# Expert slots of 128 rows against 48 whole slots and 20 slots of four 32-row pieces, in an attention-like block with a routed feed-forward part on one core

## The reference, cut to what matters

```python
logits = hidden @ router_w.T                         # 16 experts
top_vals, top_idx = jax.lax.top_k(logits, 1)         # one expert for each token
scores = sigmoid(top value at the chosen expert, -inf elsewhere)
routed_in = hidden[None] * scores.T[:, :, None]
gate, up = split(einsum('nth,nhf->ntf', routed_in, gate_up_proj))   # 128 + 128 columns
routed_out = einsum('ntf,nfh->nth', up * silu(gate), down_proj)
shared = silu(hidden @ shared_gate_w.T) * (hidden @ shared_up_w.T) @ shared_down_w.T   # width 512
out = x + shared + routed_out.sum(axis=0)
```

## Time and profile before

| | |
|---|---|
| median of 3 runs | 490.7 us (490.6 to 490.88) |
| the profiled execution | 490.73 us, span 488.6 us |
| TensorE's mean granted clock | 0.999 |
| TensorE, VectorE, ScalarE, GpSimd busy | 98%, 76%, 66%, 72% of the span |
| HBM | 21.69 MB read, 17.93 MB written |

### The profile page before, as it was taken

The page is one execution under the profiler, slowest core; times in us unless marked ns, Lnnn a source line. Parts: engine busy times, 40 slices in busy tenths (PEclk is TensorE's granted clock), DMA queues, the critical chain, the costliest instruction groups (busy, mean ns, idle before and its releaser), DMA issues.

```text
span 488.6 us, 10463 instructions
## 1 busy us (share of the span) xinstructions
PE 477.0 (98%) x3093; PEld 388.2 (79%) x3093; DVE 371.1 (76%) x1056; ACT 323.8 (66%) x623; POOL 352.3 (72%) x573
## 2 busy tenths in 40 slices
PE   8999999999999999999999999999999999999995
PEld 7655777868777778686777867888899999999995
DVE  7889899899999998997899989747445555555535
ACT  2667887978978879777687886554365555555521
POOL 6655688898888988986788777677236676667750
PEclk9999999999999999999999999999999999999999
DMA  7007001102101011020101101111389854442028
GB/s 238 2 1 281 22 12 56 54 13 66 33 34 65 24 45 54 12 67 21 46 25 41 45 1 44 45 44 37 117 197 225 226 158 136 145 139 76 24 52 294
DMA packets 33031, 39.33 MB, mean 80 GB/s; under 512 B 4913, under 2 KB 29113, under 8 KB 32720
## 3 DMA queue, kind: packets, MB, share of 16 engines
q1 hardware_dynamic: 26640, 24.98, 17.8%
q0 software_dynamic: 5760, 13.16, 7.8%
q10 hardware_dynamic: 576, 0.52, 0.3%
HBM read 21.69 MB, written 17.93 MB: 81 GB/s over the span
## 4 chain that ended last, share of the span: by engine, by line
PE 77%; DVE 6%; issue 5%; POOL 5%; DMA 4%; ACT 2%; SPq 1%; POOLq 0%; DVEq 0%; ACTq 0%
PE bank L427 17%; PE bank L420 9%; PE bank L444 6%; PE bank L414 4%; PE bank L822 3%; PE bank L823 3%; PE bank L815 3%; PE bank L435 3%; PE bank L528 3%; PE bank L514 3%; PE bank L540 3%; PE bank L524 3%; PE bank L519 3%; PE bank L688 2%; PE bank L697 2%
## 5 line engine op out<-in xcount | busy, mean ns | idle before, releaser
L427 PE MATMUL bank<-hT,wm 128*128 128x256 f32 x512 | 124.7, 383 | 0.6 <-ACT kr L908 0.6
L427 PEld LDWEIGHTS bank<-hT,wm 128*128 128x128 f32 x512 | 92.0, 190 | 18.7 <-issue 8.3
L1528 POOL DMA_INDIRECT sorted_rows<-rows,posi x64 | 71.9, 1124 | 19.6 <-issue 16.9
L1612 POOL DMA_INDIRECT out<-shared x55 | 53.2, 967 | 37.3 <-DVE shared L1442 22.3
L420 PEld LDWEIGHTS bank<-wm,k 128*128 128x128 f32 x512 | 61.7, 192 | 7.6 <-issue 6.6
L420 PE MATMUL bank<-wm,k 128*128 128x128 f32 x512 | 62.1, 275 | 0.0
L1084 ACT ACTIVATE er<-bank 128x256 f32<-128x256 f32 x40 | 15.4, 384 | 44.8 <-PE bank L823 44.3
L1450 DVE TENSOR_TENSOR e<-er,bank 128x256 f32<-128x256 f32 x40 | 16.9, 421 | 23.0 <-ACT er L1084 21.1
L444 PE MATMUL bank<-wm,actA 128*128 128x128 f32 x240 | 32.9, 280 | 0.0
L1612 POOL DMA_INDIRECT out<-rows x24 | 23.1, 964 | 11.3 <-DVE rows L1442 5.3
L944 ACT ACTIVATE h<-rows,smE 128x128 f32<-128x128 f32 x64 | 26.3, 482 | 6.7 <-POOL smE L1504 6.7
(11 more groups left out here) (256 smaller groups left out, 1293.9 us busy)
## 6 DMA issues: line engine op xcount, KB each, us to landing
shared<-sorted_rows SPq DMA_DIRECT2D x56, 128.5 KB, 2.9
shared<-x SPq DMA_DIRECT2D x16, 256.0 KB, 3.0
rows<-sorted_rows SPq DMA_DIRECT2D x24, 128.5 KB, 2.5
wexp<-w_exp SPq DMA_DIRECT2D x2, 1536.0 KB, 8.4
sorted_rows<-filler SPq DMA_DIRECT2D x17, 128.5 KB
shared<-out SPq DMA_DIRECT2D x6, 256.0 KB, 4.7
out<-shared SPq DMA_DIRECT2D x12, 128.0 KB, 2.7
sorted_rows<-rows,posi POOLq DMA_INDIRECT x64
```

Source lines behind the costliest of these rows:

```text
L427: ins = mm(dst[:, j * HALF:(j + 1) * HALF], W(name, 2 * pair_ + j), src[:, half * HALF:(half + 1) * HALF], start=True, stop=True)
L1528: g_.indirect_dma_start(sorted_ap, bass.IndirectOffsetOnAxis(posi[t % 3][:, g:g + 1].bitcast(U32), 0), rows[t % 3][:, g, :], None).then_in ...
L1612: g_.indirect_dma_start(out, bass.IndirectOffsetOnAxis(xr[k % RING][:, j, D:D + 1].bitcast(U32), 0), xr[k % RING][:, j, D + 1:ROW], None, ...
```

## The change

The slots become 68. An expert's whole slots of 128 rows come first, 48 in all, over the experts in order; what is left of an expert (whole slots beyond the 48 too) is cut into pieces of 32 rows, 80 in all, and four pieces, of whichever experts, make one slot. Two such slots make a mixed pair; pairs 5, 8, ..., 32 of the 34 are mixed.

In a mixed pair each piece has its own copy of weights (8 for a pair, not 2). Gate and up become one product for a piece, with the piece's 32 transposed tokens as the stationary operand and the 256 weight columns as the moving one, into the piece's 32-row strip of the bank. The activation then has tokens on its rows, so TensorE transposes it (2 transposes a pair, one turn behind gate and up), VectorE copies it back, and the down product is again one product for a piece, with 32 columns of activation. SP loads a mixed pair with 8 loads of 32 rows.

The rest follows from this: 23 buffers hold weight copies, ScalarE makes about four copies a turn, two on each side of its silu; the tables are a chain of 18 operations and 4 more for the fillers' places, and 14 constants for them are worked out by VectorE ahead of `z` of tile 2; two constants go. The fillers are five stores of 128 rows by GpSimd behind its last scatter, and SP waits for all of them ahead of the load of pair 5. 22 late steps, not 16, run in the last three turns.

```diff
+SUB = P // 4
+UNI = NTOK // P - NE
+SUBS = NTOK // SUB + NE - 4 * UNI
+NS = UNI + SUBS
+MIXED = range(5, 34, 3)
+NP = UNI // 2 + len(MIXED)
...
-        xw = [q, an, xn2T, th, rv]
-        XW = len(xw)
+        xw = q + an + xn2T + th + rv + k2 + a + xa + kr[2:4] + h
...
-        TAB_ROWS = 15
+        TAB_ROWS, TAB_FILL = 18, 4
+        FILLERS = NE * SUB // P + 1
-        STEPS_BEFORE, LATE_TURN, LATE_AFTER = 1, 4, 16
-        GU_BEHIND, DN_BEHIND = 1, 3
+        STEPS_BEFORE, LATE_TURN, LATE_AFTER = 1, 4, 22
+        GU_BEHIND, AT_BEHIND, DN_BEHIND = 1, 2, 3
...
+        def copied(m):
+            return min(copies_to(NP - 1), max(copies_to(min(m, NP - 1)), 4 * (m + 1))) if m >= 0 else 0
...
             for k in range(NP):
-                if k in FILL_PAIRS:
-                    sp.dma_start(sorted_ap[bass.ds(tails[k - FILL_PAIRS[0]], P), :], filler[:, :]).then_inc(s["fill_out"], 16)
+                if k == MIXED[0]:
+                    sp.wait_ge(s["fill_out"], 16 * FILLERS)
+                if first % LOADED == 0 and first >= UNI:
+                    sub_rows[:] = entries(SP_ENGINE, row_i, first, FILL_ROW, LOADED)
...
+                    if k in MIXED:
+                        for c in range(4):
+                            sp.dma_start(xr[k % RING][c * SUB:(c + 1) * SUB, j, :],
+                                         sorted_ap[bass.ds(sub_rows[entry(k, j, c) % LOADED], SUB), :]).then_inc(s[loaded(k)[0]], 16)
...
                 for k in pair(m, DN_BEHIND):
                     wait(pe, "xact", k)
+                    wait(pe, "xaT", k)
                     wait(pe, "xy", k - 2)
+                    for j in range(2):
+                        for c in range(parts(k)):
+                            rows_ = slice(c * SUB, (c + 1) * SUB) if k in MIXED else slice(0, P)
+                            ins = mm(grp(XDN_B[k % 2], j)[rows_, :], grp(xact[k % 4], j)[:, rows_], w_of(k, j, c, 2),
+                                     start=True, stop=True)
...
+                for k in pair(m, AT_BEHIND):
+                    if k in MIXED:
+                        pe.wait_ge(s["xact"], k + 1)
+                        for j in range(2):
+                            ins = nc.tensor.transpose(grp(XDN_B[k % 2], 2 + j), grp(xact[k % 4], j), ident[:, :])
+                        ins.then_inc(s["xAT"], 1)
...
+                        if k in MIXED:
+                            for c in range(4):
+                                rows_ = slice(c * SUB, (c + 1) * SUB)
+                                ins = mm(XGU_B[k % 2][rows_, j * 2 * P:(j + 1) * 2 * P], xhT(k, j)[:, rows_], gate_up_of(k, j, c),
+                                         start=True, stop=True)
...
             def one_turn(m):
-                for k in pair(m, W_BEHIND):
+                copy_weights(copied(m - 1), (copied(m - 1) + copied(m)) // 2)
                 if m < NP:
                     for u, step in late_steps(m):
                         late_step(u, step)
...
+                copy_weights((copied(m - 1) + copied(m)) // 2, copied(m))
...
                 for t in at(2):
+                    if t == 2:
+                        table_consts()
...
+                for k in pair(m, AT_BEHIND):
+                    if k in MIXED:
+                        dve.wait_ge(s["xAT"], MIXED.index(k) + 1)
+                        v.tensor_copy(xact[k % 4][:, :], XDN_B[k % 2][:, 2 * P:4 * P]).then_inc(s["xaT"], 1)
...
+            gp.wait_ge(s["tab"], TAB_ROWS + TAB_FILL)
+            for d in range(FILLERS):
+                g_.indirect_dma_start(sorted_ap, bass.IndirectOffsetOnAxis(tail_i[:, d:d + 1].bitcast(U32), 0),
+                                      filler[:, :], None).then_inc(s["fill_out"], 16)
```

More of the change, by code:

```diff
@@ L117, in wait, with grp @@
                 eng.wait_ge(s[name], (count - 1) * PER[name] + (PER[name] if k is None or t not in of else k))
+        def grp(tile, g):
+            return tile[:, g * P:(g + 1) * P]
         wm = sb("wm", MAIN_COLS)
@@ L168, in program @@
         oh = ring("oh", 2, (G, NE), BF16)
[L170 to L173, removed]
+        start_of = sb("start_of", (2, NE))
+        cnt_i, blocks_i, blocks, ahead = sb("cnt_i", (2, NE), I32), sb("blocks_i", (2, NE), I32), sb("blocks", (2, NE)), sb("ahead", NE)
+        cum, whole, rest, left = sb("cum", 1 + 2 * NE), sb("whole", NE + 1), sb("rest", NE), sb("left", NE)
+        step_of, sums, sum2 = sb("step_of", 2 * NE), sb("sums", (2, 2 * NE)), sb("sum2", 2)
+        is_sub, sub4, sub16, place_a, place_b, place_u = (sb(n, 1) for n in ("is_sub", "sub4", "sub16", "place_a", "place_b", "place_u"))
+        place16, place4 = (grp(xa[0], i).rearrange("p (w k) -> p w k", k=PACK) for i in range(2))
+        place = sb("place", WORDS)
         rowm, eidc = sb("rowm", 1), sb("eidc", 1)
         eid_i, row_i = sb("eid_i", WORDS, I32), sb("row_i", NS, I32)
-        tail_i = sb("tail_i", NE, I32)
+        in_piece, piece_no, pick, pick_no = sb("in_piece", 1), sb("piece_no", 1), sb("pick", 4), sb("pick_no", 4)
+        tails = sums[:, 0, 0:NE].rearrange("p (d c) -> p d c", c=4)
+        tail, tail_i = step_of[:, 0:4], cnt_i[:, 0, 0:5]
         def halves(*bufs):
@@ L802, in one_turn @@
                     wait(pe, "xhT", k // 2 - 1)
-                    for i in [i for i in range(4) if i % 2 in stores(k + i // 2)]:
+                    for i in range(4):
                         if i % 2 == 0:
@@ L1068, in _, with copy_weights @@
             wait(act_e, "e", NT)
+            wait(act_e, "hs", NT)
             for u, step in late_order()[1:STEPS_BEFORE]:
                 late_step(u, step)
-            def one_turn(m):
-                for k in pair(m, W_BEHIND):
-                    wait(act_e, "xDN", k - XW)
-                    for j in range(2):
-                        af(xw[k % XW][j][:, 0:EW], wexp[:, bass.ds(expert_of(words, 2 * k + j) * EW, EW)], ACT.Copy).then_inc(
-                            s["xw"], 1)
+            def copy_weights(first, last):
+                for i in range(first, last):
+                    k, j, c = copy_of(i)
+                    if i >= len(xw):
+                        wait(act_e, "xDN", copy_of(i - len(xw))[0])
+                    af(xw[i % len(xw)][:, 0:EW], wexp[:, bass.ds(expert_of(words, entry(k, j, c)) * EW, EW)], ACT.Copy).then_inc(s["xw"], 1)
+            def one_turn(m):
+                copy_weights(copied(m - 1), (copied(m - 1) + copied(m)) // 2)
                 if m < NP:
@@ new lines, in tables @@
+                tab(v.tensor_tensor_scan(ahead[:, :], one16[:, :], blocks[:, 0, :], 0.0, ALU.mult, ALU.add))
+                tab(v.tensor_scalar(cum[:, 1:1 + NE], ahead[:, :], float(UNI), None, ALU.min))
+                tab(v.tensor_tensor(whole[:, 0:NE], cum[:, 1:1 + NE], cum[:, 0:NE], ALU.subtract))
+                tab(v.scalar_tensor_tensor(rest[:, :], whole[:, 0:NE], -4.0, blocks[:, 1, :], ALU.mult, ALU.add))
+                tab(v.tensor_tensor_scan(cum[:, 1 + NE:1 + 2 * NE], one16[:, :], rest[:, :], float(UNI), ALU.mult, ALU.add))
```

166 lines of the change are left out of this document (92 added, 74 removed).

## The result

The changed kernel takes 495.34 us (median of four runs, 494.54 to 495.68); the kernel before took 490.79 us beside it. The ratio is 1.0091 with an interval of 1.0079 to 1.0103: 4.5 us slower, where the forecast had 2.8. The profiled execution took 495.68 us with a span of 493.9, 5.3 us more than before's 488.6. Where they lie is found by following landmarks of TensorE through both traces: the last block of logits, the late step of turn 4, the last down product and the end.

What follows compares the result with a forecast made beforehand. TensorE, full nearly everywhere, was taken to bound the kernel. The terms 0.2 + 1.7 - 0.3 + 1.9 + 0.8 - 1.5 sum to +2.8, so 490.73 us becomes 493.5 us, range 488.5 to 498.5.

Steps and rivals of the forecast that it cites:

- TensorE's work, +0.2: Expert stage: 39.5 pairs at 61.2 us become 24 whole and ten mixed pairs at 61.4 us, +0.2 us.
- the transposes of the activation, +0.8: Turn behind gate and up: TensorE waits for the activation in two turns without a late step, +0.8 us (0 to 1.6).
- The logits' row: Logits before the change: four 32-column products run at once, with 0.14 standing, 0.10 lost going in and 0.10 coming out.
- The packing rule of the Trainium skill: Mixed pairs: a packed group costs one product plus about 4 ns per further tile, making TensorE's term -5.7 us.
- Constants, +1.7: VectorE ahead of z of tile 2: 14 chained operations take 3.1 to 3.4 us, +1.7 us (0.5 to 2.2).
- the 0.3 for those removed: Start, VectorE running without a pause: two constants of some 0.2 us each go, -0.3 us (0 to -0.46).
- TensorE's wait for h: Tile 0, at 49.27 us: the 0.43 us wait for ACT's h was to grow by over 1 us.
- Tables and load, +1.9: Tables and pair 5's first mixed load behind the fillers: TensorE waits longer, +1.9 us together (0.4 to 3.5).
- The end, -1.5: Last 20 us: 19 late steps cover reading the late rows back; pause and part of the queue go, -1.5 us (0 to -2).
- Faster without the price of the strips: Rival, mixed pairs: the strips' fixed price isn't paid at neighbouring blocks, 10 x 0.68 us less, 486.8 us; chance 0.13.
- The two waits are covered: Rival: the constants fall into slack and the first mixed load lands in time, 490.3 us; chance 0.15.
- ScalarE did not slip: Rival, expert stage: silu comes 0.6 us late at the other eight mixed pairs, +4.8, 498.3 us; chance 0.12.

Runs made afterwards that it cites:

- the later down product: Changed kernel with the down product of a slot issued one turn later, so down blocks stand next to gate-and-up blocks: 492.94 us, ratio 1.0042.
- the combined kernel with 16: Changed kernel with constants one a round, first mixed pair in turn 6, down product one turn later, and 16 late steps, not 22: 493.02 us, ratio 1.0046.

## Why the prediction was right, and where its terms were off

**Right: slower, for the reasons named, within the range.** The strips' saving is paid back by the way in and out; the constants and the first mixed load make the loss. That the time lies inside the range is not owed to errors that cancel: by the table of stretches, one term was 2.4 us too low, and the others were off by at most half a microsecond. The range itself was wide, 10 us.

*TensorE's work, +0.2, and the transposes of the activation, +0.8:* together +1.0 measured. The blocks took 1.15 to 1.20 and 0.77 us. The two waits for an activation came, 0.3 us each; the remaining 0.4 us were not split further. The logits' row, one short block, gave the price of a longer one rightly, and the later down product shows what it is made of. The packing rule of the Trainium skill ("TensorE: Matmul & The Clock Gate", Part 3, "Measured speedup vs the span model"), weighed in the prediction, leaves out that price; the trace has it.

*Constants, +1.7, the term that failed in size:* 3.8 us came in place of 1.4 (1.7 less the 0.3 for those removed, which showed as no gain: with the constants spread, the first logits still come 0.2 us after before's). Three things were missed. The fourteen took 4.28 us, not about 3.3, as three of them ran beside GpSimd's scalings and sum and took 1.6 us more for it, 1.15 of that in one operation. The forecast priced them by a chain in a stretch where GpSimd had no such operation, only its scatters. Hardly any of that time was covered: z was 3.23 us late, h 3.4, and the 1.19 us of idle time was all the slack there was. And "many are one column wide, so I take less" held for those (0.19 us from start to start, not 0.24), but what GpSimd added outweighed it, so the upper bound of 2.2 was passed as well. One sign that the forecast named did not show: TensorE's wait for h did not grow by over 1 us, it vanished, as TensorE came later itself. It stood 2.47 us for the squares instead, ten microseconds ahead of h, and lost its clock; both, which the forecast didn't name, are worth about 0.5 us of the 3.8 beyond what h would have cost.

*Tables and load, +1.9:* +2.4. The wait was where it was named. The fillers landed at 360.8, not 356: some 3.8 of these 4.8 us are the start's delay, which TensorE shares, and 1.1 the slower landing (5.27 instead of 4.12).

*The end, -1.5:* -1.9. That 19 steps cover the reading back is right, and 16 need not (the combined kernel with 16). But in the changed kernel 16 did it too, and by the count of the table above that run has 20.5 us behind its last down product (472.79 to 493.3), against 20.1 with 22 steps and 22.0 before: most of the gain there is not the six steps'. The last stores were nearer to the last product (the reading back is issued 5.5 us behind it with 22, 5.1 with 16, 6.0 before); whether that is all was not tried. (By the prediction's own rates its 8 gate and 11 down steps take 24.2 us, not 23.7; nothing in its sum hangs on that.)

*The rivals.* Faster without the price of the strips: the price is real, but it can be shared, and that, with the two waits taken away, gives 488.5 us: a different kernel, and no support for the rival. "The two waits are covered", 490.3 us: they weren't, but the run in which they are taken away has 490.06. ScalarE did not slip; no wait of TensorE for a silu or a copy shows in the middle of the stage. With the first mixed pair in turn 6 one copy is late, by 0.39 us.

## What to carry to other kernels

A block of small instructions in a full pipeline seems to cost by what it exceeds the slack of the engines behind it: 4.2 us in one place cost 3 us, in either of two rounds, while the same instructions in two blocks (2.9 us in all, as none met GpSimd's sum) or one a round cost under half a microsecond. Price such instructions with what the neighbouring engine does beside them. Column tiles on TensorE have a price for each change between tiles and whole products, here 0.34 us a block for going in and out; order the work so that packed blocks stand together before judging whether packing pays. A load that hangs on a late store needs a turn of its own between its issue and its use, and a cover that just suffices in one kernel fails in another.

## What was not expected of the hardware

A VectorE operation on 128 x 4 numbers took 1.30 us beside a GpSimd sum of 1.27, and 0.16 in another round; an addition on 128 x 16 took 1.20 beside such a sum, 0.39 beside GpSimd's scalings and 0.16 where the constants are spread. GpSimd's sum was not lengthened (1.27 and 1.26, before 1.28). TensorE's granted clock fell after waits of 2.5 and of 1.95 us (0.74 and 0.66 in the 5 us that hold most of it), and 24 passes took 4.44 instead of 2.84 us; yet keeping it up in the first case won 0.5 us only, as another engine was late as well. In the second it was not tried.
